# Gate logits as four plain fp32 products instead of twelve split ones, in a kernel of local attention and a mixture of experts

## What is computed

```
x = x + attention(layernorm(x))         # 16 heads of 8, window of 64, softmax
x = x + ffn(layernorm(x))

# in ffn, x2 is the second normalised input, 128 channels:
logits = x2 @ gate_kernel               # (tokens, 128) @ (128, 16): this is what changes
scores = sigmoid(logits)
# best 2 of 4 groups, best 4 of 16 experts, weights normalised, times 2.5
y = sum over the 4 experts: weight * (silu(x2 @ w_gate[e]) * (x2 @ w_up[e])) @ w_down[e]
y = y + shared expert of x2
```

## Time and profile before

| | us |
|---|---|
| median of 3 runs | 743.44 |
| the profiled execution, its own time | 743.04 |
| span of its trace | 741.1 |
| TensorE matmul busy | 695.4 (94%) |
| ScalarE busy | 535.5 (72%) |
| VectorE busy | 508.4 (69%) |
| GpSimd busy | 454.1 (61%) |

### The profile page before, as it was taken

How to read it: one execution, slowest core, us unless ns; L and a number is a source line. 1 busy time by engine, 2 the same in 40 slices (tenths; PEclk the granted TensorE clock), 3 DMA queues, 4 the chain that set the end, 5 groups by cost and what they waited for, 6 DMA issues and landing times.

```text
span 741.1 us, 19372 instructions
## 1 busy us (share of the span) xinstructions
PE 695.4 (94%) x6264; PEld 568.0 (77%) x6264; DVE 508.4 (69%) x1588; ACT 535.5 (72%) x1603; POOL 454.1 (61%) x561
## 2 busy tenths in 40 slices
PE   3778889999999999999999999999999999999997
PEld 1667668888887878788787878788888878778775
DVE  2456585868677685867677685867768585876564
ACT  3675778787777878787878779787877878764332
POOL 6233156767777676767767676767767576445433
PEclk9998899999999999999999999999999999999999
DMA  5010013040413123040313113040313213041321
GB/s 167 1 30 11 20 62 99 28 130 20 127 45 115 57 72 100 17 129 26 117 54 114 58 60 112 5 138 28 115 57 102 69 50 108 3 128 32 115 73 43
DMA packets 50243, 52.58 MB, mean 71 GB/s; under 512 B 5664, under 2 KB 31904, under 8 KB 50080
## 3 DMA queue, kind: packets, MB, share of 16 engines
q1 hardware_dynamic: 50208, 52.14, 22.7%
HBM read 43.20 MB, written 4.72 MB: 65 GB/s over the span
## 4 chain that ended last, share of the span: by engine, by line
PE 75%; ACT 9%; DVE 9%; issue 4%; DMA 1%; POOL 1%; DVEq 0%; POOLq 0%; ACTq 0%; SPq 0%
PE PS L940 11%; PE PS L1007 11%; PE PS L819 11%; PE PS L857 10%; PE PS L821 10%; PE PS L820 10%; ACT probs L579 5%; PE PS L845 3%; PE PS L970 3%; DVE neg_max L736 2%; PE PS L953 2%; DVE tu L728 2%; PE PS L1004 2%; PE PS L1024 1%; ACT q_by_head L531 1%
## 5 line engine op out<-in xcount | busy, mean ns | idle before, releaser
L579 ACT ACTIVATE probs<-PS,neg_max 128x96 f32<-128x96 f32 (+1 forms) x1024 | 247.3, 350 | 90.9 <-DVE neg_max L736 90.9
L460 POOL TENSOR_TENSOR gate<-gate,spread 128x512 f32<-128x512 f32 x124 | 158.6, 1279 | 166.4 <-ACT gate L531 88.8
L728 DVE SCALAR_TENSOR_TENSOR tu<-th,PS 128x512 f32<-128x512 f32 x128 | 87.5, 683 | 100.9 <-ACT th L547 70.9
L1007 PE MATMUL PS<-wd,hh 128*128 128x128 f32 x1024 | 136.4, 276 | 4.4 <-DVE hh L788 2.2
L736 DVE TENSOR_REDUCE neg_max<-PS 128x4 f32<-128x384 f32 (+1 forms) x256 | 122.3, 516 | 21.6 <-PE PS L857 17.0
L1007 PEld LDWEIGHTS PS<-wd,hh 128*128 128x128 f32 x1024 | 126.8, 192 | 12.1 <-DVE hh L788 4.9
L465 POOL TENSOR_TENSOR hh<-gate,tu 128x512 f32<-128x512 f32 x100 | 127.9, 1279 | 7.8
L819 PE MATMUL PS<-x_hi,w_hi 128*128 128x512 f32 x288 | 124.6, 433 | 0.2 <-DVE tu L728 0.2
L821 PE MATMUL PS<-x_lo,w_hi 128*128 128x512 f32 x288 | 114.4, 397 | 0.0
L714 DVE STREAM_TRANSPOSE probsT<-probs 128x768 f32<-128x768 f32 (+1 forms) x128 | 114.4, 893 | 0.0
L857 PE MATMUL PS<-k_by_row,q_by_head 64*128 64x192 f32 (+2 forms) x1024 | 113.9, 327 | 0.0
(11 more groups left out here) (106 smaller groups left out, 963.7 us busy)
## 6 DMA issues: line engine op xcount, KB each, us to landing
spread<-weights_by_expert SPq DMA_DIRECT2D x248, 128.0 KB, 2.9
X<-x SPq DMA_DIRECT2D x32, 256.0 KB, 3.2
OUT<-H SPq DMA_DIRECT2D x16, 256.0 KB, 3.1
out<-OUT SPq DMA_DIRECT2D x16, 256.0 KB, 2.9
ffn_stage<-w_gu SPq DMA_DIRECT2D x1, 1152.0 KB, 5.7
wd<-w_down SPq DMA_DIRECT2D x1, 512.0 KB, 6.6
weights_by_expert<-cT SPq DMA_DIRECT2D x16, 32.0 KB, 1.6
probsT<-w_att SPq DMA_DIRECT2D x1, 192.0 KB, 2.7
```

What stands on the lines that cost most here:

```text
L460: tt(gate2[:, :], gate[:, k % 2, :], spread[:, k % SP_BUFS, :], ALU.mult).then_inc(s_g2, 1)
L579: ins = nc.scalar.activation(probs[:, u % 2, tt, 2 * rows + e, j0:KW], PS[:, rows, n * KW + j0:n * KW + KW], ACT.Exp, bias=neg_max[:, rows ...
L728: v_.scalar_tensor_tensor(tu[:, k % 2, :], th[:, :], 1.0, PS[:, 5, :], ALU.add, ALU.mult).then_inc(s_tu, 1)
L1007: ins = mm(PS[:, 7, r], hh[:, k % 2, r], wd[:, k, :], start=(k == 0 and n == 0), stop=(k == NP - 1), skip_group_check=True)
```

## The change

ScalarE copies the transposed bank into a new fp32 buffer `x2_f` (128x512, one for all groups) instead of into `x2_hi`. VectorE rounds it from there into `x2_hi` with a copy that changes the type (a CAST), waits for it, and subtracts with both operands in SBUF. The logits are four fp32 products of `x2_f` and of the fp32 gate weights, which already lie in `ffn_stage`.

```diff
-ORDER_PER_SLOT = 5
+ORDER_PER_SLOT = 7
...
+        x2_f = sb("x2_f", [P, TOK])
...
                     g, b = at(sl, s, XT2, 4, GB)
                     if g:
                         side, bank = filled(act, sl, s, LATE)
-                        copy(x2_hi[:, g.par, T * b:T * b + T], bank[:, 0:T]).then_inc(s_high[side], 1)
+                        copy(x2_f[:, T * b:T * b + T], bank[:, 0:T]).then_inc(s_high[side], 1)
...
                         side, bank = high_out(sl, s, LATE)
                         cols = slice(T * b, T * b + T)
-                        split_low(x2_lo[:, g.par, cols], bank[:, 0:T], x2_hi[:, g.par, cols]).then_inc(s_taken[side], 1)
+                        link(sl, v_.tensor_copy(x2_hi[:, g.par, cols], x2_f[:, cols]))
+                        split_low(x2_lo[:, g.par, cols], x2_f[:, cols], x2_hi[:, g.par, cols]).then_inc(s_taken[side], 1)
...
                         for n in range(NT):
                             r = slice(P * n, P * n + P)
-                            ins = exact3(bank[:, E * n:E * n + E], x2_hi[:, g.par, r], x2_lo[:, g.par, r],
-                                         *w2(GK, E))
+                            ins = mm(bank[:, E * n:E * n + E], x2_f[:, r], ffn_stage[:, 0:E], start=True, stop=True)
                         ins.then_inc(s_filled[side], 1)
```

## The result

| | us |
|---|---|
| before, median of 6 runs | 742.50 |
| changed, median of 6 runs (775.45 to 781.88) | 776.64 |
| ratio, 95% interval | 1.047 (1.044 to 1.050) |
| changed, the profiled execution: its own time, its span | 776.01, 774.2 |

It is slower, as forecast, but by 34 us where 23.7 were forecast, and outside the range (751 to 773).

The account below looks back on a forecast made before the run. TensorE, busy 94% of the span, was taken to bound the kernel, with no cover ahead of the logits. 12.6 us there, 10.1 ahead of the values product and 1.0 elsewhere added 23.7 to 743.04: 766.7 us, range 751 to 773.

Parts of the forecast that it names:

- The saving: Logits on TensorE: four fp32 products take 0.89 us instead of 1.34 for twelve, saving 0.45 us a group, 7.2 in all.
- The port: VectorE and GpSimd share SBUF ports under an exclusive lock, so both new instructions wait for GpSimd; chance 0.71.
- step 7: Ahead of the logits: subtraction waits behind `hh`, logits start 1.42 us later, net 0.97 us, 13 times, 12.6 us.
- Step 3: Ahead of the values product: CAST waits for `hh`, `x_lo` 1.02 us later, TensorE held 0.84 us, 12 times, 10.1 us.
- The slot of 43.7 us: Sign that the forecast is right: a slot takes 43.7 us in place of 41.9.
- The rest of the ends: Logits and `x_lo` in the filling and draining slots, outside the counted places: +1.0 us together.
- moves along: Behind the logits: `tu` waits for the gate product through ScalarE, so it shifts with TensorE and the 0.97 us stays.
- No blocking: Rival: the CAST runs unhindered; logits -0.07 us, values product 0.20 later; 744.4 us, no change; chance 0.08.
- the subtraction keeping the port: Rival: ahead of the logits the subtraction holds off `hh`, so only step 3 costs; 753.2 us; chance 0.12.
- four weight loads a product: Rival: fp32 logits take 1.79 us, 0.90 more than forecast, 16 times; 781 us; chance 0.04.
- miss its gap in step 7: Case: the CAST also goes behind `hh`, 0.3 us more, 13 times; 770.6 us, within the forecast's own spread.
- The faster one: Rival: `x_lo` isn't later, so the logits' saving counts whole; needs 0.4 us slack ahead of them; 735.8 us; chance 0.05.

Follow-up runs that it names:

- the two filler kernels: Changed kernel with six constant products ahead of the logits' wait, 764.7 us; the same with the old twelve split products for the logits, 771.7 us.
- e7: Kernel before plus ScalarE's copy into x2_f ahead of x2_hi; four fp32 logits products waiting for x2_f alone, VectorE as it was; 732.7 us, ratio 0.986.
- e1: Changed kernel with VectorE's CAST and subtraction both reading the PSUM bank; 747.2 us, ratio 1.005.
- e2: Changed kernel with the subtraction reading the PSUM bank, the CAST still reading SBUF; 754.4 us, ratio 1.015.
- e6: Changed kernel whose logits wait for ScalarE's copy into x2_f, no longer for the subtraction's x2_lo; 741.6 us, ratio 0.997.
- e3: Changed kernel with the CAST reading the PSUM bank, the subtraction still reading SBUF; 776.8 us, ratio 1.044.
- e5: Changed kernel with the old twelve split products for the logits in place of the four; 789.7 us, ratio 1.064.

## Why the prediction was right in its parts and wrong in its sum

- **What bounds the kernel: right.** The chain's row of 0.14 us between `x_lo` and the logits said that there was no cover, and the experiment that takes this wait away alone moved 35 us.
- **The saving: right.** 0.45 us a group forecast, 0.44 measured by the two filler kernels.
- **The port: right, in kind and in size.** Forecast for step 7: the CAST done 0.14 us behind line 460's end, the subtraction 0.28 behind `hh`; seen: 0.16 and 0.27. Step 3: the CAST about 1.0 us, TensorE held 0.84; seen: 0.99 and 0.80. The counts of 13 and 12 held as well: 13 subtractions took 1.43 to 1.44 us, and 12 CASTs of step 3 took 0.96 to 1.04. One sign was off by its own sum: 0.19 us of idle time and 1.42 more are 1.6 ahead of the logits, not "some 1.8"; seen were 1.46 to 1.58. The forecast of the port came from two groups of rows at the kernel's very start and end, and the earlier trace rows, neither near the change.
- **The slot of 43.7 us: right** for six of 12 slots, and for all of them once the gap is filled. The rest of the ends came to 2.5 us with a fall of the clock in them; 1.0 and the 13th logits' 0.97 were forecast.
- **The step that failed** is the one under "Step 7", that TensorE's 0.97 us behind "moves along" and is all: "nothing there catches up". Nothing caught up, but I took every instruction behind the wait at its price of before, at the full clock. TensorE's idle time there went from 0.19 us in the rows of before to some 1.5, and in half of the slots the granted clock then fell to 1.2 GHz: 1.5 us more each, seven times in the profiled execution, 10.5 us. That execution is 33.0 us above the one of before, 9.3 more than the 23.7 of the sum, and the falls are more than all of it. The sum had no term for them, and the range, whose upper end was made of the port's variants alone, had no room.
- **The rivals.** No blocking, the subtraction keeping the port, and four weight loads a product (the logits took 0.92 us, not 1.79) are all refuted. The CAST didn't miss its gap in step 7 (0.30 to 0.32 us in 12 of the 13 places, 0.44 in one). The faster one needed slack ahead of the logits; there was none. Waiting for what is read takes the place of slack, and with step 3 undisturbed as well (e7) it gains 10.6 us, 0.86 in each slot of the loop.

## What to carry to other kernels

Before moving a VectorE operation's source from PSUM to SBUF, look at what GpSimd does at that moment: here a copy within SBUF, or a second SBUF operand, stood until the end of a GpSimd instruction of 1.3 us, and took 1.0 and 1.4 us in place of 0.3 and 0.4. When an instruction stops reading a tensor, move its wait too: here the wait for `x2_lo` outlived the reading of it, and moving it took back 35 us. And where an edit lengthens TensorE's idle time beyond what the trace has shown, the price of the idle time alone isn't the upper end; add a stretch at half the clock behind it, which cost 1.5 us a time here.

## What the runs showed that I had not expected

- An idle time of 1.46 to 1.58 us on a TensorE that is busy 94% of a slot (42.43 of 45.18 us, 40.93 of 43.72) was followed by a stretch at 1.2 GHz in six of 12 slots, and in ten of 12 in the kernel where the subtraction alone reads SBUF. Shorter ones, 0.45 to 0.65 us ahead of the logits in the loops of e1 and e2, whose subtraction reads PSUM, were followed by none there, and neither were the 0.8 us ahead of the values product in e6. What decides between the slots that fall and those that don't stays open. The runs of the three kernels whose clock falls in the loop and whose logits wait for the long subtraction (changed, e3, e5) lie 6.2 to 8.3 us apart, those of the others 1.7 to 3.4; that the number of falls differs from run to run would explain it, but only one run of each has a trace.
- A CAST of 128x256 from SBUF to fp32r in SBUF takes 0.28 us at its shortest, where nothing is in its way, against 0.42 from PSUM. Of e1 and e2, which differ in this instruction's source alone, the one with the CAST that can be faster is the slower kernel, by 7 us: it isn't undisturbed in step 3.
